# Splitting half of the second layer's products of the late blocks, with a rebuilt beginning, in a fused cross-attention and expert-feed-forward kernel

## The reference, cut to what matters

```
lat = layer_norm(_layernorm(x), g_l, b_l);  c = layer_norm(ctx, g_m, b_m)
q = lat @ Wq;  k, v = split(concat([c, lat], 1) @ Wkv)       # 16 heads of 64
x = x + softmax(q k^T / 8) v @ Wout
# feed-forward: 8 experts, each token takes the one with the largest score
z = _layernorm(x);  e = argmax(z @ centroids.T)
h = relu(w1[e] @ (xhat * ln_g[e] + ln_b[e]) + b1[e])          # 1024 features
y = z + w2[e] @ h + b2[e]
out = x + sigmoid(z . centroids[e]) * y + (1 - sigmoid(...)) * z
```

## Time and profile before

| | before |
|---|---|
| median of 3 runs | 1076.86 us |
| the profiled execution | 1074.92 us, of which 1073.1 us are the span of its instructions |
| granted TensorE clock, mean | 0.996 of full speed |
| PE busy | 1055.8 us (98%) |
| DVE, ACT, POOL busy | 799.1 (74%), 670.1 (62%), 491.3 (46%) us |
| DMA share of q1 (SP's queue) | 61.0% of 16 engines |

### The profile page before, as it was taken

The page is one execution under the profiler, slowest core; times in us unless marked ns, Lnnn a source line. Parts: engine busy times, 40 slices in busy tenths (PEclk is TensorE's granted clock), DMA queues, the critical chain, the costliest instruction groups (busy, mean ns, idle before and its releaser), DMA issues.

```text
span 1073.1 us, 24076 instructions
## 1 busy us (share of the span) xinstructions
PE 1055.8 (98%) x8456; PEld 945.9 (88%) x8456; DVE 799.1 (74%) x1905; ACT 670.1 (62%) x1819; POOL 491.3 (46%) x640
## 2 busy tenths in 40 slices
PE   7899999999999999999999999999999999999998
PEld 6779888989898888889898988888888999999997
DVE  6786888888888988898888888898886554454441
ACT  5674766575757667675657575676665645666551
POOL 1563555546464644555454646455454342222222
PEclk9999999999999999999999999999999999999999
DMA  5466676765758575767667585756467757776770
GB/s 181 113 159 159 154 192 166 189 167 153 203 138 209 149 193 141 186 171 190 164 170 183 144 219 137 204 145 148 95 165 218 256 169 243 254 235 226 230 256 29
DMA packets 159660, 190.51 MB, mean 178 GB/s; under 512 B 17453, under 2 KB 149037, under 8 KB 154672
## 3 DMA queue, kind: packets, MB, share of 16 engines
q1 hardware_dynamic: 155088, 179.09, 61.0%
q0 software_dynamic: 3360, 8.53, 2.2%
q10 hardware_dynamic: 1088, 1.31, 0.3%
HBM read 65.72 MB, written 46.07 MB: 104 GB/s over the span
## 4 chain that ended last, share of the span: by engine, by line
PE 93%; DVE 2%; POOL 1%; DMA 1%; ACT 1%; issue 1%; SPq 0%; ACTq 0%; POOLq 0%; DVEq 0%
PE psum L689 16%; PE psum L722 16%; PE psum L864 12%; PE psum L759 11%; PE psum L849 10%; PE psum L738 9%; PE psum L774 9%; PE psum L708 8%; PE psum L777 1%; DMA w_ring<-in_w_q 1%; POOL prob L1639 1%; DMA prob_t<-prob 1%; DVE neg_max L1265 0%; POOL w_o_lo L1693 0%; ACT prob L1018 0%
## 5 line engine op out<-in xcount | busy, mean ns | idle before, releaser
L1639 POOL TENSOR_TENSOR prob<-prob,inv_sum 128x512 f32<-128x512 f32 x176 | 182.5, 1051 | 205.9 <-DVE inv_sum L1271 205.9
L1018 ACT ACTIVATE prob<-psum,neg_max 128x256 f32<-128x256 f32 x352 | 164.4, 481 | 46.9 <-DVE neg_max L1265 38.3
L1265 DVE TENSOR_REDUCE neg_max<-psum 128x2 f32<-128x512 f32 x256 | 162.3, 674 | 35.8 <-PE psum L738 35.8
L864 PE MATMUL psum<-w,v_n 128*128 128x256 f32 x608 | 134.2, 379 | 0.0
L1277 DVE STREAM_TRANSPOSE prob<-prob 128x512 f32<-128x512 f32 x176 | 121.5, 699 | 9.5 <-POOL prob L1639 8.9
L864 PEld LDWEIGHTS psum<-w,v_n 128*128 128x128 f32 x608 | 114.2, 190 | 14.8
L1639 POOL TENSOR_TENSOR w_ring<-w_ring,inv_sum 128x512 f32<-128x512 f32 x76 | 78.1, 1041 | 78.8 <-DVE inv_sum L1271 78.4
L1025 ACT ACTIVATE head_out_hi<-psum 128x512 fp32r<-128x512 f32 x52 | 31.3, 601 | 117.0 <-PE psum L759 103.4
L1710 POOL DMA_INDIRECT out<-x_in,r_ring x38 | 39.9, 1049 | 127.8 <-DVE x_in L1506 127.4
L1008 ACT ACTIVATE v_n<-psum 128x512 f32<-128x512 f32 x128 | 78.3, 612 | 21.0 <-PE psum L722 21.0
L997 ACT ACTIVATE k_hi<-psum 128x512 fp32r<-128x512 f32 x128 | 77.3, 604 | 21.9 <-PE psum L689 18.9
(11 more groups left out here) (185 smaller groups left out, 2711.0 us busy)
## 6 DMA issues: line engine op xcount, KB each, us to landing
sorted_rows<-filler SPq DMA_DIRECT2D x54, 660.0 KB
prob_t<-prob SPq DMA_DIRECT2D x176, 128.0 KB, 2.8
w_ring<-prob SPq DMA_DIRECT2D x176, 128.0 KB
w<-in_experts SPq DMA_DIRECT2D x19, 1024.0 KB
w_ring<-in_experts SPq DMA_DIRECT2D x18, 1024.0 KB, 5.8
prob_t<-w_ring SPq DMA_DIRECT2D x76, 128.0 KB, 2.8
w_ring<-w_ring SPq DMA_DIRECT2D x76, 128.0 KB
w_ring<-normed SPq DMA_DIRECT2D x56, 128.0 KB, 3.0
```

Of the source, the lines that this page charges most:

```text
L864: last = pe.matmul(bank[:, 0:d_model], hid[:, s % 2, f, i * P:(i + 1) * P], w2[:, f * d_model:(f + 1) * d_model], start=(f == 0), stop=(f ...
L1018: act.activation(prob_at(u, bb)[:, :, parity, i], scores_i, ACT.Exp, bias=neg_max[:, at, i:i + 1], accum_out=prob_sum[:, at, i:i + 1]).the ...
L1265: dve.tensor_reduce(neg_max[:, (4 * u + n) % 8, :], psum[:, n, :].rearrange("p (i j) -> p i j", i=2), AXIS_X, ALU.max, negate=True).then_i ...
L1639: pool.tensor_tensor(probs, probs, inverse, ALU.mult).then_inc(s_soft, 1)
```

## The change

**In the late blocks' second layer** (slots 4 and up, `FIRST_SPLIT = 4`) four of the eight pieces of 128 hidden features are multiplied in parts, four stay plain. ACT puts the first four pieces in `hid_raw`, DVE splits them (`split_hidden`), ACT makes the high part of half of w2 (inside `relu_parts`), POOL the low part (`low_weights_2`). They live in freed tiles of the attention. `finish` writes its first result into `fin` and not into a tile of its own.

**SP's order in the late loop**: the two weight loads come ahead of the vectors and rows; w2 and b2 of block 5 are loaded before the loop.

**In the beginning** the normalisation goes a side at a time (context first), the high parts are made from PSUM directly, the first keys' matmuls go in the order of their operands, one value is made between queries and scores of step 0, two after them, and the fourth after the queries of step 1.

```
@@ bank_order: order of the PSUM banks, the same as PE's order below
@@ block.sync
+                load_weights_2(n_early - 1)
+                load_b2(n_early - 1)
                 scattered(n_batches)
                 run = block_steps(sp, count_empty(sp))
                 for s in range(n_early, n_slots + 1):
-                    run(s, (load_vectors,), (load_rows,), (load_weights_1,))
-                    run(s - 1, (load_weights_2,), (load_b2,))
+                    run(s, (load_weights_1,))
+                    if s > n_early:
+                        run(s - 1, (load_weights_2,))
+                    run(s, (load_vectors,), (load_rows,))
+                    if s > n_early:
+                        run(s - 1, (load_b2,))
                     run(s, (move_rows,))
@@ block.tensor
+                def layer_2_split(s):
+                    pe.wait_ge(f_w2h, s - FIRST_SPLIT + 1)
+                    pe.wait_ge(f_w2l, s - FIRST_SPLIT + 1)
+                    pe.wait_ge(f_hl, FS // 2 * (s - FIRST_SPLIT + 1))
+                    pe.wait_ge(f_ha, FC // 2 * s)
+                    def in_parts(bank, i, first):
+                        for n, (hw, hx) in enumerate(PASSES):
+                            for f in range(FS):          # FS = 4
+                                last = pe.matmul(bank, hid_hl[hx][:, s % 2, f, i * P:(i + 1) * P], w2_hl[s % 2][hw][:, f, :], ...
+                    def plain(bank, i, first):
+                        for f in range(FS, FC): ...      # FC = 8
+                    in_parts(bank, 0, True); plain(bank, 0, False)
+                    plain(bank, 1, True);    in_parts(bank, 1, False)
-                warm(3)
-                first_keys(0)
-                first_keys(1)
+                warm(2)
+                first_keys()
                 weights_split(Q_FIRST)
                 queries(0)
+                weights_split(V_FIRST)
+                values(0, 0, 0)
                 for u in range(n_steps):
                     scores(u)
                     if u == 0:
-                        weights_split(V_FIRST)
-                        for bb in range(2):
-                            for side in range(2):
-                                values(0, bb, side)
+                        values(0, 0, 1)
+                        values(0, 1, 0)
                         weights_split(K_REST)
...
+                    if u == 0:
+                        values(0, 1, 1)        # behind queries(1)
...
-                    layer_2(s)
+                    if s < FIRST_SPLIT:
+                        layer_2(s)
+                    else:
+                        layer_2_split(s)
@@ block.scalar
+                def relu_parts(s):
+                    b1 = vec_ring[:, s % NR, 2 * KC:]
+                    if s == FIRST_SPLIT:
+                        wait_low(act, n_pairs - 1, 1)
+                    for i in range(FC // 2):
+                        act.wait_ge(f_h, FC // 2 * (s - 1) + i + 1)
+                        if i < FS // 2 and s > FIRST_SPLIT:
+                            act.wait_ge(f_hl, FS // 2 * (s - 1 - FIRST_SPLIT) + i + 1)
+                        elif i == FS // 2:
+                            wait_made(act, ("fy", s - 2, 1))
+                        for f in (2 * i, 2 * i + 1): ...    # Relu into hid_raw or hid_plain
+                        if i == 1:
+                            act.wait_ge(f_w2[s % NW2], 16 * (s // NW2 + 1))
+                            ...
+                            act.activation(w2_hl[s % 2][0], w2_ring[s % NW2][:, 0:FS * d_model]..., ACT.Copy).then_inc(f_w2h, 1)
@@ block.vector
+                def split_hidden(s):
+                    for i in range(FS // 2):
+                        dve.wait_ge(f_ha, FC // 2 * (s - 1) + i + 1)
+                        ...
+                        then_next(dve.tensor_copy(hi, hid_raw[:, i, :]))
+                        dve.tensor_tensor(lo, hid_raw[:, i, :], hi, ALU.subtract).then_inc(f_hl, 1)
-                    run(s + 2, (transpose_rows,), (low_weights_1,), (split_xn,))
+                    run(s + 2, (transpose_rows,))
+                    run(s + 1, (split_hidden,))
+                    run(s + 2, (low_weights_1,), (split_xn,))
                     run(s, (finish,))
+                layer_norm_stats(0, 0); layer_norm_stats(0, 1); first_variances(0)
+                layer_norm_stats(0, 2); layer_norm_stats(0, 3); first_variances(1)
+                first_shifts(0)
+                low_weights(K_FIRST)
+                first_shifts(1)
+                first_normalised()
+                first_inputs()
                 low_weights(Q_FIRST)
+                low_weights(V_FIRST)
                 low_keys(0, 0)
@@ block.gpsimd
+                def low_weights_2(s):
+                    pool.wait_ge(f_w2h, s - FIRST_SPLIT + 1)
+                    raw = w2_ring[s % NW2][:, 0:FS * d_model].rearrange("p (f d) -> p f d", f=FS)
+                    pool.tensor_tensor(w2_hl[s % 2][1], raw, w2_hl[s % 2][0], ALU.subtract).then_inc(f_w2l, 1)
-                pool.wait_ge(s_var, 1)
-                pool.tensor_tensor(ln_scale[:, 0, :], var_eps[:], minus_half[:], ALU.pow).then_inc(s_pow, 1)
+                for side in range(2):
+                    part = slice(2 * side, 2 * side + 2)
+                    pool.wait_ge(s_var, side + 1)
+                    pool.tensor_tensor(ln_scale[:, 0, part], var_eps[:, part], minus_half[:, part], ALU.pow).then_inc(s_pow, 1)
                     if s in the late loop:
                         run(s + 2, (add_base,))
+                        run(s + 1, (low_weights_2,))
                         write_rows(s)
```

More of the change, by code:

```diff
@@ L52, in bank_order @@
         if u == 0:
-            order += [("v", 0, side, half) for side in range(2) for half in range(2)]
+            order += [("v", 0, 0, 1), ("v", 0, 1, 0)]
         if following:
@@ L175, in build @@
             k_s = [sbuf(a, f"k_{h}", [P, 2, 2, BANK], F32R) for h in ("hi", "lo")]
+            FS = FC // 2
+            with ExitStack() as late:
+                hid_hi = sbuf(late, "hid_hi", [P, 2, FS, BLOCK], F32R)
+                sbuf(late, "hid_between", [P, 3 * FS * BLOCK])
+                hid_lo = sbuf(late, "hid_lo", [P, 2, FS, BLOCK], F32R)
             v_n = sbuf(a, "v_n", [P, 2, 2, 2, BANK])
@@ L867, in layer_2 @@
                         last.then_inc(f_y, 1)
+                def layer_2_split(s):
[6 more added lines that the diff above has]
+                            for f in range(FS):
+                                last = pe.matmul(bank, hid_hl[hx][:, s % 2, f, i * P:(i + 1) * P], w2_hl[s % 2][hw][:, f, :],
+                                                 start=(first and n == 0 and f == 0), stop=(not first and n == 2 and f == FS - 1))
+                        return last
+                    def plain(bank, i, first):
+                        for f in range(FS, FC):
+                            last = pe.matmul(bank, hid_plain[:, s % 2, f - FS, i * P:(i + 1) * P],
+                                             w2_ring[s % NW2][:, f * d_model:(f + 1) * d_model],
+                                             start=(first and f == FS), stop=(not first and f == FC - 1))
+                        return last
+                    bank = begin(("fy", s, 0))[:, 0:d_model]
+                    in_parts(bank, 0, True)
+                    plain(bank, 0, False).then_inc(f_y, 1)
+                    bank = begin(("fy", s, 1))[:, 0:d_model]
+                    plain(bank, 1, True)
+                    in_parts(bank, 1, False).then_inc(f_y, 1)
                 pe.wait_ge(s_blank, 1)
@@ L992, in gain_bias, with first_inputs @@
                     last_reads(item, last)
+                def first_inputs():
+                    item = ("ln", 0, 0)
+                    wait_made(act, item)
+                    for c in range(KC):
+                        last = act.activation(kv_t[0][:, c, 0:2, 0:P],
+                                              work_bank(number[item])[:, 2 * c * P:2 * (c + 1) * P].rearrange("p (b t) -> p b t", b=2),
+                                              ACT.Identity, bias=ln_w[:, 1, c:c + 1], scale=ln_w[:, 0, c:c + 1])
+                    last.then_inc(s_hi_first[0], 1)
                 def high_keys(u, i):
@@ L1245, in layer_norm_stats, with first_variances, first_shifts, first_normalised @@
                     dve.bn_aggr(mean_var[:, j, :], stats[:, j, :]).then_inc(s_mv, 1)
[L1247 to L1255, removed]
-                    dve.scalar_tensor_tensor(out=shift, in0=mean, scalar=-1.0, in1=scale, op0=ALU.mult, op1=ALU.mult).then_inc(s_lnp, 1)
+                def first_variances(side):
+                    part = slice(2 * side, 2 * side + 2)
+                    var = mean_var[:, part, 1]
+                    dve.wait_ge(s_mv, 2 * side + 2)
+                    if side == 0:
+                        dve.tensor_scalar(var_eps[:, part], var, EPS, None, ALU.add).then_inc(s_var, 1)
+                    else:
```

(9 more changed lines are left out.)

117 lines of the change are left out of this document (77 added, 40 removed).

## The result

The changed kernel takes 1097.97 us in the median of 4 runs (1093.58 to 1100.14), beside 1077.53 us for the kernel before on the same chip (1076.63 to 1078.94): ratio 1.0186, 95% interval 1.0154 to 1.0218. The forecast was 1098.7, 21.8 above the 1076.86 it started from; the measured rise is 20.4. The profiled execution took 1100.14 us, its span is 1098.3.

A forecast was written before the change was run, and what follows sets the result against it. PE bounds the kernel (busy 98%), with SP's load loop hidden behind it. The profiled 1074.92 us + 25.8 (late part) - 4 (beginning) = 1096.7, and 1.94 to the median gives 1098.7 us, range 1082 to 1112.

The forecast's parts named there:

- The deciding step: Late loop: rows issued behind w1 and w2 land at M + 10.3, making the period 15.25 us, not 12.66.
- The queue is served in order: SP's load queue: rows issued behind 2 MB of weights land only when those are through, 5.9 us at 353 GB/s.
- the bound: Late period: 12.4 us if rows land after 2.8 us regardless, 16.2 if the queue moves 2.1 MB a sixth slower.
- The slack of 2 us: Old late loop of SP, ACT and DVE: 10.5 us without its delay, 2 us less than PE's period.
- PE's holes: Late blocks: PE idle some 3 us ahead of each first layer.
- The second layer: Blocks 4 to 18, half in parts: 6.33 us against 6.91, PE saving 0.58 a block, 8.7 in all.
- The beginning: Steps 0 and 1: values fill PE's gaps, normalisation goes a side at a time; -4 us, bounds -1 and -6.
- Its term for the clock: Beginning, after the second gap: with the gap mostly filled PE's clock may not fall, 0 to -1.7 us.
- The end chain: From block 18's normalisation to PE's end: 8.6 us, first layer 5.75, two second layers 2 x 6.33; together 27.0.
- the clock falls too: Rival: PE's late idle time lowers its clock; only the last block pays, 1.7 or 3.4 us: 1101 us; chance 0.13.
- the queue is no hindrance: Faster rival: weights leave room for the rows, late loop 12.4 us, time 1064.5 us; chance 0.12.
- The beginning brings nothing: Rival: POOL takes the beginning's gain back, time 1102.7 us; chance 0.08.

The follow-up runs named there:

- the version with one MB ahead: Changed kernel with SP's late loads reordered to w1, vectors, rows, w2 of the block before, b2: 1067.54 us, ratio 0.9906 to the kernel before.
- the fastest version: Changed kernel with SP's order w1, vectors, rows, w2, b2 and w2's low part made by DVE, not POOL: 1063.48 us, ratio 0.9886 to the kernel before.

## Why the prediction was right, point by point

**The deciding step, the loop over SP's loads, held.** From the end of the moved rows, M = 976.55: w1 at M + 0.8 (forecast 1.27), then 1.14 (1.10), 1.14 (1.10) and 1.09 (1.15): the rows go out at M + 4.1, forecast 4.6. They are used at M + 10.0, forecast 10.3. The step of 1.6 + 0.75 + 2.6 for normalising, transposing and copying comes out at 988.97 - 986.59 = 2.4 for the first two, as DVE follows ACT at once, and 2.5. Period 14.96 against 15.25: 3.5 us less over twelve blocks. The 0.3 us that I had added for the last share of the load had no row behind it, and the measured time has no need of it.

**Its stated reason held only in part.** "The queue is served in order" was what I took from b2's packets. The loads on ACT's queue land as late, though nothing but 6 KB is ahead of them there, so order within SP's queue can't be all of it; 2 MB that are with the engines first delay what comes behind from either queue. Counted from the end of the moved rows they are used at M + 10.1 there and M + 10.0 here, which is why the number survived. Of the bound only the lower end, 2.8 us to landing, was read from a row; the upper one, a sixth slower, was not. The nearest row was block 3's, 6.6 us: there w1 had gone out too, at 827.49, 1.1 us ahead of the w2 in the earlier trace rows, so it was already a case of 2 MB ahead. Here it is 5.9.

**The slack of 2 us was not borne out.** The 10.5 us of the old loop leave out that the vectors wait for an output to land. With the old order and PE's own sum at 12.08 the normalisations come 12.94 and 12.81 us apart, and SP waits for the scatters for 14.8 and 17.6 us in all; whether this is the whole difference wasn't shown. In the changed kernel this wait does not occur in the late blocks, so the forecast didn't suffer from it.

**PE's holes are smaller than the 3 us forecast:** 22.8 us of waits over the twelve blocks from 880 to 1060 us, 1.9 a block. Part of the room went to first layers that ran at a lower clock, below.

**The second layer** takes 6.33 us a block as forecast: two of them lie at the end of the chain as 1.44 + 3.46 + 2.87 + 3.46 + 1.44 = 12.67.

**The beginning was right in itself, and misplaced in the sum.** The scores of step 1 come at 28.89, 4.8 us earlier than the earlier trace rows (4.3 in the beginning alone), and the experiment gave 4.9 by the medians against a forecast of 4. Its term for the clock, 0 to 1.7, was not part of it: the half clock had cost nothing by step 2. But the sum let it reach block 6 whole. Block 6's normalisation is 0.9 earlier only (881.57 against 882.47), 3.1 us lost. I had written that no weights but its own were ahead of its rows, and that the vectors wait for an output to land; I didn't ask what that landing would share the engines with. SP's one long wait there, and its issues:

```profile
SPq L510 <- DMA out<-x_in,r_ring: 6.2, 1, 6.2
```

```profile
866.31 0.34 SPq L504 DMA_DIRECT2D w<-in_experts  x1
...
869.57 0.01 SPq L497 DMA_DIRECT2D w_ring<-in_experts  x1
876.73 0.33 SPq L512 DMA_DIRECT2D vec_ring<-in_experts  x1
```

POOL issues the second scatter at 868.86, and the vectors go out 7.9 us later (7.9 to 8.0 in all four versions in which w1 of block 6 goes ahead of them). With w1 behind the rows but block 5's w2 still ahead it is 5.9 to 6.6 us in three versions, and 3.9 to 4.1 in the two versions with the beginning alone, where neither is ahead. The old order in the changed kernel differs in nothing else and has block 6 normalised at 878.37, 3.2 us earlier than here; with the low part on DVE it is 879.33. So SP's order accounts for 2 to 3 us of the 3.1, partly in the scatter's landing and partly in that of the rows.

**The end chain was 3.4 us too short,** 30.4 us from the end of block 18's normalisation to PE's end and not 27.0. The chain shows both parts (start, us, what):

```profile
1067.35 4.46 DVE w_lo L1591
1071.81 0.35 DVE k_hi L1585
...
1072.98 7.46 PE psum L873 x48
```

First, 10.3 us and not 8.6 to the first layer: the list of the tail left w1's low part out, and it takes 4.46 us, where 13 of them took 2.29 us each before (29.8 us in all). POOL's new subtraction stands beside it:

```profile
1066.94 2.72 POOL L1835 TENSOR_TENSOR w_o_lo<-w,w_o_hi 128x1024 fp32r<-128x1024 f32 x1 [1.88 <-ACT w_o_hi L1213]
```

It ends at 1069.66, and 2.29 more make 1071.95, where DVE's instruction was followed by the next at 1071.81. The rule is in the Trainium skill, SBUF - State Buffer, section on two separate sides: a DVE instruction with two SBUF inputs and a POOL instruction that reads SBUF lock each other out, the second waiting for the first. The trace agrees to 0.14 us, here and in ten of the twelve blocks from 880 to 1060 us, in which POOL started first as well. I had costed "the low part on POOL" at nothing. In the version with one MB ahead POOL's subtraction mostly comes after DVE's, and only two of 13 take 4.4 to 4.5 us; so most of the mean comes back with the order, and the rest with the low part on DVE:

```profile
L1591 DVE TENSOR_TENSOR w_lo<-w_ring,w_hi 128x2048 fp32r<-128x2048 f32 x12 | 49.1, 4094 | 0.0
```

```profile
L1589 DVE TENSOR_TENSOR w_lo<-w_ring,w_hi 128x2048 fp32r<-128x2048 f32 x13 | 34.0, 2617 | 0.0
```

```profile
L1589 DVE TENSOR_TENSOR w_lo<-w_ring,w_hi 128x2048 fp32r<-128x2048 f32 x13 | 29.7, 2283 | 0.0
```

(the changed kernel, the version with one MB ahead, then the fastest version, all from 880 to 1060 us).

Second, the last first layer takes 7.46 and not 5.75, as the clock fell behind 2.6 us without a matmul; first layers that follow such a gap at full clock take 5.99, so the clock's share is 1.5:

```profile
1070.00:1074.00 4.00, 1.36 (x12) 1.18 (x11) 3.86 (x6) 0.00 (x0) 0.00 (x0) 1.00 0.46 184
1074.00:1078.00 4.00, 4.00 (x23) 4.00 (x22) 1.74 (x4) 1.40 (x4) 2.12 (x2) 0.57 0.13 44
```

So the rival "the clock falls too" held in its part that costs, once, with 1.5 us for the forecast 1.7. Its sum was slightly off: 1098.7 with 1.7 to 3.4 more is 1100.4 to 1102.1. By the rule cited with it the clock would fall in all twelve periods; it fell in the first layers of six of the 13 blocks from 6 to 18 (they took 7.4 to 8.6 us, the others 6.0). The row of the beginning, which the prediction called such a case, was one wait for DVE and no loop with a DMA. In the late blocks the clock was low too (0.95 over 958 to 1060 us, and 0.57 from 968 to 972), and cost nothing there, as forecast, for the loop and not PE sets the period. The kernel with the new order and plain second layers has a mean clock of 0.994, this one 0.987.

**The sum.** PE ends at 1093.1; the forecast, with the beginning, is 1094.1 - 4 = 1090.1. The 3.0 us between them are -3.5 (period) + 3.1 (beginning) + 3.4 (end chain). Behind PE's end another 0.4 us were added, so the profiled execution took 1100.14 and not 1096.7, 3.4 more. That the median is off by 0.7 only is luck of a last term: I added 1.94 us from the profiled execution to the median, and here the profiled execution is 2.2 above the median. The mechanism was right to 3 us in 21, with three terms that partly cancelled.

**Of the rivals,** "the queue is no hindrance" was wrong for this order, but its sum, 1064.5, is close to what the kernel gives when both hindrances are taken away (1063.48, with one MB ahead and w2's low part on DVE; 1067.54 with the order of one MB ahead alone). "The beginning brings nothing" is refuted for the beginning itself (ratio 0.9941), but in this kernel three quarters of it is lost before block 6 is normalised.

## What to carry to other kernels

When a change shortens the engine that bounds the kernel, write down the next loop's period before anything else: here it seemed to have 2 us of slack, and one reordering of prefetches ahead of a small load on that loop made its turn 15.0 us, where PE had set 12.5. Look for every wait of that loop, those for outputs to land too. In this kernel what mattered is how many bytes are with the DMA engines when the small load on the path is issued, and not which of the two queues it sat on; one MB behind it and one MB ahead was better than two on either side, as scatters have to land as well. And a subtraction handed to POOL "for nothing" can be paid by DVE: 4.46 us for 2.29, in 11 of the 13 late blocks of the changed kernel, where POOL started first.

## What the runs showed of the hardware that was not expected

- POOL's 128x256 multiplication by a scalar (`base`) has a mean of 550 ns in the late part before and 677 in the changed kernel, 1517 and 1448 in the versions with the old order and with one MB ahead, and 1969 and 1911 in the same two with w2's low part on DVE. One more subtraction on DVE thus adds 0.5 us. The rest of the rise comes neither with the order alone (the kernel before has the old one) nor with the split alone (the changed kernel has it), and was not taken apart; where the multiplication falls beside DVE's work may decide it. A pair of them beside DVE's two subtractions of weights took 4.83 us (old order, low part on DVE):

```profile
951.62 4.83 POOL L1833 TENSOR_SCALAR base<-r_ring 128x256 f32<-128x256 f32 x2 [4.50 <-DMA out<-x_in,r_ring]
```

```profile
951.47 2.28 DVE L1588 TENSOR_TENSOR w_lo<-w_ring,w_hi 128x2048 fp32r<-128x2048 f32 x1
953.67 1.22 DVE L1603 TENSOR_TENSOR head_out_lo<-w,head_out_hi 128x1024 fp32r<-128x1024 f32 x1
```

- The same subtraction of 128x1024 takes 1.22 us on DVE and 2.3 to 2.9 on POOL, there beside a busy DVE.
- An idle gap of 2.03 us on PE was followed by half clock at 33.66 us in the kernel before, and not at 31.54 us in the one with the values in their old place, with the same work behind it and since the scores of step 0 (13.5 us in both), though not ahead of that. Within the changed kernel a first layer behind a gap of 2.17 us (968.01) took 7.48 us, and one behind 2.52 us (1027.62) took 5.99. The length of the gap alone doesn't tell whether the clock falls.
